# Experts' output products with the weights stationary, and gates spread over partitions through memory

## The reference, cut to what matters

```python
# layer 1: 8 experts, 64 -> 256 -> 64, each token goes to one expert, with a capacity
y = sum over e of gate1[t, e] * (relu(x @ w1[e] + b1[e]) @ w2[e])  +  gate1[t] @ b2
# NaN and infinities of y are replaced, then x = layer_norm(x + y)
# a two-layer gated recurrence along the 64 tokens of a row, x = layer_norm(x + h)
# layer 2: 16 experts, 64 -> 128 -> 64, each token goes to its two best experts
y = sum over e of gate2[t, e] * (relu(x @ w1[e] + b1[e]) @ w2[e])  +  gate2[t] @ b2
# x = layer_norm(x + layer_norm(x + y) * gamma + beta)
```

## Time and profile before

| | |
|---|---|
| Time before, median of 3 runs | 3099.89 us (3096.33 to 3101.36) |
| The profiled execution | 3111.34 us, span 3109.5 us |
| PE busy | 2843.0 us (91%) |
| PE weight loads busy | 1838.0 us (59%) |
| DVE busy | 2121.2 us (68%) |
| ACT busy | 2004.1 us (64%) |
| POOL busy | 61.8 us (2%) |
| Granted TensorE clock, mean | 0.962 of full speed |

### The profile page before, as it was taken

How to read it: one execution, slowest core, us unless ns; L and a number is a source line. 1 busy time by engine, 2 the same in 40 slices (tenths; PEclk the granted TensorE clock), 3 DMA queues, 4 the chain that set the end, 5 groups by cost and what they waited for, 6 DMA issues and landing times.

```text
span 3109.5 us, 78718 instructions
## 1 busy us (share of the span) xinstructions
PE 2843.0 (91%) x30194; PEld 1838.0 (59%) x30194; DVE 2121.2 (68%) x4213; ACT 2004.1 (64%) x2417; POOL 61.8 (2%) x81
## 2 busy tenths in 40 slices
PE   5777789999889999889999779999999999999997
PEld 3444456666656666556666534444444437888886
DVE  6999668888658888668888534445445435757855
ACT  5888656777546777556777457777777774444531
POOL 0000000000000000000000020000000001000000
PEclk9999899999999999999999889999999999999965
DMA  3432347644436654546544424111111100000000
GB/s 100 123 116 94 115 146 227 212 174 173 154 129 222 205 182 177 161 151 220 200 175 180 140 63 96 58 48 48 58 48 48 58 0 1 1 1 4 1 4 7
DMA packets 110842, 335.82 MB, mean 108 GB/s; under 512 B 46774, under 2 KB 74710, under 8 KB 74838
## 3 DMA queue, kind: packets, MB, share of 16 engines
q1 hardware_dynamic: 88150, 161.45, 16.6%
q10 hardware_dynamic: 18432, 134.23, 10.6%
q0 software_dynamic: 4096, 37.75, 5.7%
HBM read 179.24 MB, written 154.14 MB: 107 GB/s over the span
## 4 chain that ended last, share of the span: by engine, by line
PE 79%; DVE 7%; issue 6%; ACT 5%; DMA 2%; ACTq 0%; SPq 0%; DVEq 0%
PE pA L1436 15%; PE pA L1444 8%; PE pT L1531 8%; PE pS L1473 7%; PE pD L1520 4%; PE pD L1487 4%; PE pD L588 4%; PE pT L1462 3%; PE pA L588 3%; PE pD L1407 3%; PE pD L1502 3%; PE pS L574 2%; PE pT L574 2%; DVE arena L1803 2%; PE pA L1462 2%
## 5 line engine op out<-in xcount | busy, mean ns | idle before, releaser
L1770 DVE TENSOR_REDUCE small<-arena 128x32 f32<-128x1056 f32 x320 | 396.5, 1241 | 322.1 <-ACT arena L1605 318.6
L1436 PEld LDWEIGHTS pA<-conv_bd,h_in 128*128 128x128 f32 x4096 | 481.6, 193 | 108.1 <-issue 108.1
L1436 PE MATMUL pA<-conv_bd,h_in 128*128 128x128 f32 x4096 | 520.2, 281 | 2.0 <-DVE arena L1763 1.7
L1595 ACT COPY w_sb<-pA 128x1024 f32<-128x1024 f32 x256 | 259.4, 1013 | 251.8 <-PE pA L1444 233.6
L1616 ACT ACTIVATE h_new<-pT,bet,gam 128x1024 f32<-128x1024 f32 x256 | 307.1, 1199 | 155.2 <-PE pT L1462 138.2
L1784 DVE SCALAR_TENSOR_TENSOR w_sb<-w_sb,small 128x1024 f32<-128x1024 f32 x320 | 385.5, 1209 | 2.1
L1605 ACT ACTIVATE arena<-w_sb 128x1024 f32<-128x1024 f32 x320 | 338.6, 1058 | 10.2
L1473 PEld LDWEIGHTS pS<-cst,h_new 128*128 128x128 f32 x2048 | 222.5, 142 | 205.4 <-issue 132.7
L1462 PE MATMUL pT<-cst,w_sb 128*128 128x128 f32 x2048 | 280.4, 282 | 38.1 <-DVE w_sb L1784 20.3
L1473 PE MATMUL pS<-cst,h_new 128*128 128x128 f32 x2048 | 282.9, 282 | 25.2 <-ACT h_new L1616 22.6
L1462 PEld LDWEIGHTS pT<-cst,w_sb 128*128 128x128 f32 x2048 | 234.9, 145 | 103.7 <-DVE w_sb L1784 49.2
(11 more groups left out here) (300 smaller groups left out, 3919.2 us busy)
## 6 DMA issues: line engine op xcount, KB each, us to landing
h_scratch<-h_new ACTq DMA_DIRECT2D x128, 1024.0 KB, 4.4
h_in<-h_scratch SPq DMA_DIRECT2D x128, 1024.0 KB, 5.0
y_scratch<-w_sb POOLq DMA_DIRECT2D x32, 576.0 KB, 8.5
y_in<-y_scratch SPq DMA_DIRECT2D x512, 36.0 KB
w_sb<-in_L_tok_w1r_dram POOLq DMA_DIRECT2D x8, 576.0 KB, 6.9
w_sb<-in_L_tok_w1i_dram POOLq DMA_DIRECT2D x8, 576.0 KB, 6.8
w_sb<-in_L_tok_w2r_dram POOLq DMA_DIRECT2D x8, 576.0 KB, 7.0
w_sb<-in_L_tok_w2i_dram POOLq DMA_DIRECT2D x8, 576.0 KB, 6.9
```

The source lines that it names most:

```text
L1436: pe.matmul(pA[:, c:c + 128], h_in[:, 1024 * n + c:1024 * n + c + 128], conv_bd[:], start=(j == 0), stop=False, skip_group_check=True)
L1595: act.copy(raw[n], pA[:]).then_inc(s["copied"], 1)
L1770: dve.reduce_sum(var[n], sq[n % 2], axis=AX).then_inc(s["summed"], 1)
```

## The change

- `output` swaps its operands: `w2` of one block (128 x 64) is stationary, and 512 tokens of `hid` stream. The two halves k of a chunk go to partitions 0 to 63 and 64 to 127 of one bank, so the result has features on partitions. A step now covers both halves of an expert: layer 1 has 4 such products where there were 16, layer 2 has 2 where there were 8. `hidden` makes both halves in one step too, and holds 4 (layer 1) or 2 (layer 2) of the 8 `hid` buffers for each expert.
- The gate of a token must now lie along the free dimension, the same on 64 partitions. After `gt`, POOL stores the turned gates of a chunk to memory (`g1_dram`, `g2_dram`) and waits until they are there; SP then loads, for each expert, two broadcasts of 64 partitions x 512 tokens (pieces of 512 bytes) into one of 8 buffers `GB`. DVE waits for the buffer and multiplies by it. SP also loads the gates of the chunk once in compact form (`GE`) for `eb`.
- `eb` becomes two products, `b2` stationary and `GE` streaming. A new step `yb` turns the sum back to token-major with 4 transposes on PE; `post1` and `post2` read its bank. The guard moves ahead of it, onto the turned sum.
- `gru` on DVE joins two instructions into one. The stores of the results move from SP to POOL. 8 parameter loads fewer are made. `TOKEN_ORDER` is written anew.

```diff
@@ TOKEN_ORDER (start of it) @@
-    xt1.0 xt1.3 qkv.0 xt1.1 sc.0 ex.0 qkv.1 pt.0 sc.1 xt1.2 pv.0 qkv.2 ex.1 pt.1 wg.0 xt2.0 sc.2 ex.2 gl1.0 gx1.0 pt.2 pv.1 cum.0
-    pv.2 e1.0 e1.0 e1.0 e1.0 e1.0 xt2.1 e1.0 gt1.0 gl1.1 gx1.1 xt2.2 cum.1 qkv.3 gt1.1 e1.0 sc.3 e1.0 eb1.0 post1.0 e1.1 ex.3
+    xt1.0 qkv.0 xt1.1 sc.0 ex.0 qkv.1 pt.0 xt1.2 pv.0 qkv.2 xt1.3 xt2.0 sc.1 ex.1 sc.2 ex.2 gl1.0 pt.1 gx1.0 pt.2 cum.0 pv.1 qkv.3
+    gt1.0 e1.0 pv.2 e1.0 e1.0 xt2.1 e1.0 xt2.2 e1.0 e1.0 sc.3 gl1.1 e1.0 ex.3 gx1.1 e1.0 eb1.0 pt.3 wg.0 cum.1 gl1.2 yb1.0 pv.3
+    gt1.1 e1.1 e1.1 xt3.0 e1.1 gx1.2 gru0.0 xt2.3 e1.1 gru1.0 e1.1 gback.0 cum.2 e1.1 e1.1 xt4.0 gl1.3 gl2.0 gx2.0 gm2.0 e1.1
+    eb1.1 gt2.0 e2.0 e2.0 e2.0 e2.0 e2.0 e2.0 e2.0 yb1.1 e2.0 e2.0 gx1.3 e2.0 e2.0 xt3.1 e2.0 gru0.1 e2.0 cum.3 gru1.1 gt1.2 e2.0
...
+    e2.2 gl2.3 e2.2 e2.2 e2.2 gx2.3 gm2.3 e2.2 e2.2 e2.2 e2.2 gt2.3 e2.2 e2.2 eb2.2 e2.3 yb2.1 e2.3 e2.3 e2.3 e2.3 e2.3 e2.3 yb2.2
+    e2.3 e2.3 e2.3 e2.3 e2.3 e2.3 e2.3 e2.3 e2.3 eb2.3 yb2.3
@@ output, on PE @@
-                step(c, e, k, slot):
-                    for i in range(4):
-                        for h in range(H):
-                            mm = pe.matmul(b[:, S * (4 * k + i):S * (4 * k + i) + S],
-                                           hid[(slot + h) % 8][:, 128 * i:128 * i + 128], w2[:, (e * H + h) * S:(e * H + h) * S + S],
-                                           start=(h == 0), stop=(h == H - 1))
+                step(c, e, slot):
+                    for h in range(H):
+                        for k in range(2):
+                            mm = pe.matmul(b[64 * k:64 * k + 64, :], w2[:, (e * H + h) * S:(e * H + h) * S + S],
+                                           hid[(slot + H * k + h) % 8], start=(h == 0), stop=(h == H - 1))
@@ output_bias (eb) and turn_back (yb), on PE @@
-                    sent("d", pe.matmul(b[:], GT[c % 2][0:8 * E, :], b2[0:8 * E, :], start=True, stop=True))
+                    pe.wait_ge(s[f"ge{layer}{c % 2}_loaded"], 32 * (c // 2 + 1))
+                    for k in range(2):
+                        q = 64 * (c % 2) + 32 * k
+                        mm = pe.matmul(b[64 * k:64 * k + 64, :], b2[q:q + E, :], GE[layer - 1][c % 2][k][0:E, :], start=True, stop=True)
...
+                    for i in range(4):
+                        mm = pe.transpose(b[:, 128 * i:128 * i + 128], chunk(Y, c)[:, 128 * i:128 * i + 128], ident)
@@ combine, on DVE @@
-                        dve.tensor_tensor(by_tile(Z3[e % 2]), by_tile(b[:]), gv, ALU.mult).then_inc(s["td_free"], 1)
+                    dve.wait_ge(s[f"g_loaded{i % NGB}"], 32 * (i // NGB + 1))
...
+                        dve.tensor_tensor(Z3[e % 2], b[:], GB[i % NGB], ALU.mult).then_inc(s["td_free"], 1)
                         dve.tensor_tensor(y, y, Z3[e % 2], ALU.add)
@@ token_pool, for gt and yb2 @@
+                    pool.wait_ge(s["ts_free"], n_s + 4)
+                    pool.dma_start(dram[c], GT[c % 2][0:8 * E, :]).then_inc(s["gates_stored"], 16)
+                    pool.wait_ge(s["gates_stored"], 16 * GT_PLACE[int(key[0][2]), c])
...
+                    pool.wait_ge(s["acc_done"], c + 1)
+                    pool.dma_start(dst, chunk(X, c).rearrange("p (t x) -> p t x", x=S)).then_inc(s["out_stored"], 16)
@@ token_sp, for each expert and chunk in order @@
+                if (layer, c) not in begun:
+                    sp.wait_ge(s["gates_stored"], 16 * GT_PLACE[layer, c])
+                    for k in range(2):
+                        sp.dma_start(GE[layer - 1][c % 2][k][0:E, :].rearrange("e (t p) -> e t p", t=4), rows[k]).then_inc(s[f"ge{layer}{c % 2}_loaded"], 16)
+                if i >= NGB:
+                    sp.wait_ge(s["td_free"], freed[i - NGB] + 4)
+                for k in range(2):
+                    sp.dma_start(GB[i % NGB][64 * k:64 * k + 64, :].rearrange("d (t p) -> d t p", t=4),
+                                 rows[k, e].partition_broadcast(64)).then_inc(s[f"g_loaded{i % NGB}"], 16)
@@ gru, on DVE @@
-                    link(dve.tensor_scalar(GV, b[:], gbias[:, 2 * layer + 1:2 * layer + 2], 0.5, ALU.add, ALU.add))
-                    link(dve.tensor_tensor(GV, GV, GS, ALU.max))
+                    link(dve.scalar_tensor_tensor(out=GV, in0=b[:], scalar=half_bias[:, layer:layer + 1], in1=GS, op0=ALU.add, op1=ALU.max))
```

More of the change, by code:

```diff
@@ L203, in token_steps @@
             seen[op, c] = e + 1
-            units += [(int(op[1]), c, e, k) for k in range(2)]
-    slots = lambda layer: 2 if layer == 1 else 1
+            units.append((int(op[1]), c, e))
+    slots = lambda unit: 4 if unit[0] == 1 else 2
     steps, split, held, issued, out, slot = [], set(), 0, 0, 0, 0
@@ L212, in token_steps @@
             continue
[L213 to L224, removed]
+        while issued < len(units) and units[issued][0:2] in split and held + slots(units[issued]) <= 8:
+            layer, u, e = units[issued]
+            units[issued] += (slot,)
+            steps.append((f"hid{layer}", u, e, slot))
+            held += slots(units[issued])
+            slot = (slot + slots(units[issued])) % 8
+            issued += 1
+        layer, u, e, at = units[out]
+        steps.append((f"out{layer}", u, e, at))
+        held -= slots(units[out])
+        out += 1
     return steps
@@ L415, in build @@
         pick1, pick2, diff2, exp2 = ([tiny(w) for _ in range(2)] for w in (E2 * CT, E2 * CT, CT, CT))
-        inverse = tiny(CT)
+        inverse, half_bias = tiny(CT), tiny(2)
+        NGB = 8
+        GB = [w_sb[:, 2048 + 512 * i:2560 + 512 * i] for i in range(4)] + [w_sb[:, 6656 + 512 * i:7168 + 512 * i] for i in range(3)] + [h_in[:, 3584:4096]]
+        GE = [[[t[64 * j + 32 * k:64 * j + 32 * k + 32, 0:512] for k in range(2)] for j in range(2)] for t in (y_in, ge2)]
+        assert tiny_at[0] <= 6656
+        g1_dram = nc.dram_tensor("gates1_scratch", [NCH, CT * E1, P], F32, kind="Internal").ap()
+        g2_dram = nc.dram_tensor("gates2_scratch", [NCH, CT * E2, P], F32, kind="Internal").ap()
+        GT_PLACE, EB_FREED, sends_d = {}, {}, 0
+        for key in token_steps():
+            sends_d += TOKEN_SENDS.get(key[0], (0, 0))[0]
+            if key[0] in ("gt1", "gt2"):
+                GT_PLACE[int(key[0][2]), key[1]] = len(GT_PLACE) + 1
+            if key[0] in ("eb1", "eb2"):
+                EB_FREED[int(key[0][2]), key[1]] = sends_d + 4
         pA, pT, pD, pS = pb("pA"), pb("pT"), pb("pD"), pb("pS")
@@ L692, in hidden, with step, turn_gates @@
             def hidden(H, b1, **_):
[L694 to L697, removed]
+                def step(c, e, slot):
+                    for i in range(2 * H):
+                        q = e * H + i % H
+                        act.activation(hid[(slot + i) % 8], take()[:], ACT.Relu, bias=b1[:, q:q + 1]).then_inc(s["ts_free"], 1)
                 return step
-            def turn_gates(E, GT):
+            def turn_gates(layer, E, GT):
                 def step(c):
+                    if c >= 2:
+                        act.wait_ge(s["gates_stored"], 16 * GT_PLACE[layer, c - 2])
                     act.copy(GT[c % 2][0:8 * E, :], take()[0:8 * E, 0:P]).then_inc(s["ts_free"], 1)
@@ L868, in add_bias, with bias2, guard @@
                 own_freed()
-            def post1(c):
-                x, y = chunk(X, c), chunk(Y, c)
+            def bias2(c):
+                add_bias(c)
+                dve.sem_inc(s["mixed2"], 1)
+            turned = lambda b: b[:].rearrange("p (t h x) -> p t h x", h=2, x=S)
+            def guard(c):
+                add_bias(c)
+                y = chunk(Y, c)
                 I32 = mybir.dt.int32
@@ L942, in post2 @@
                 dve.sem_inc(s["acc_done"], 1)
-            do = dict(qkv=qkv, sc=sc, pv=pv, xt2=lower, xt4=lower, gl1=gl1, cum=cum, out1=combine(E1, gates1), out2=combine(E2, gates2),
-                      eb1=add_bias, eb2=add_bias, post1=post1, gru0=gru(0), gru1=gru(1), gback=gback, gl2=gl2, gm2=gm2, post2=post2)
+            do = dict(qkv=qkv, sc=sc, pv=pv, xt2=lower, xt4=lower, gl1=gl1, cum=cum, out1=combine(E1), out2=combine(E2),
+                      eb1=guard, eb2=bias2, yb1=post1, gru0=gru(0), gru1=gru(1), gback=gback, gl2=gl2, gm2=gm2, yb2=post2)
             dve.wait_ge(s["par_loaded"], 16 * N_PARAMS)
```

129 lines of the change are left out of this document (78 added, 51 removed).

## The result

The kernel before took 3098.11 us (median of 4 runs, 3092.86 to 3101.36), the changed one 3006.34 (4 runs, 2999.78 to 3009.09): a ratio of 0.9702, with a 95% interval of 0.968 to 0.9724. The profiled execution took 3009.09 us, 2.75 above the median.

A forecast was written before the change was run, and what follows sets the result against it. TensorE bound the token stage; VectorE would after the change. Start 2605 + VectorE with waits 412 + gates 6 + last store 5 = 3028 us span; + 2 - 11 = 3019, taken as 3020, range 2966 to 3086.

The forecast's parts named there:

- the forecast's own case: Token stage: cheaper output products pass the bound from TensorE to VectorE; time 3020 us, chance 0.52.
- The output products: TensorE, token stage: 1.87 us per layer-1 expert where 3.46 stood, 1.01 per layer-2 expert where 1.73 stood.
- the halves don't run side by side: Rival, output products: a pair costs 2.1 us instead of 1.73, 47 us more TensorE, about 3150 us; chance 0.03.
- The rest of an expert: Hidden products on TensorE: 0.98 us for four, 1.90 for layer 1's eight; whole experts 3.77 and 1.99 us.
- VectorE's need: Token stage from 2605 us: 329 us busy, divided by 0.92 for issue, makes 357 us.
- the prediction's own needs, 422 and 357: Token stage: TensorE's need before the change, at full clock, 422 us; VectorE's need after it, 357 us.
- The waits: Between engines in the token stage: 15% over VectorE's need as before, 357 x 1.155 = 412 us.
- The gates: Broadcast loads: hidden mid-chunk; 2 us each at three chunk starts, 6 us together, between 0 and 25.
- The rival that wanted them late for every expert: Gate loads don't overlap: 5.2 us a unit, VectorE waits for all 96, time 3113 us; chance 0.11.
- The tail: End of the kernel: POOL's last store takes between 2.6 and 8.5 us, taken as 5.
- PE cold all through layer 2: Rival: TensorE, waiting more often, runs layer 2 at 1.2 GHz, adding 125 us; time about 3081 us, chance 0.20.
- The order: Head of the token stage: `cum.0` ahead of chunk 1's attention may save up to 5 us, left as margin.

The follow-up runs named there:

- one half: Changed kernel with both halves' output products written to the same 64 partitions, instructions unchanged in number and size; 3076.76 us, 0.9914 of the kernel before.
- no low part: Changed kernel without the second hidden product of each pair (low part of the hidden weights); 3000.13 us, 0.9664 of the kernel before.
- Before, no guard: Kernel before without the guard's six instructions per chunk, which replace non-finite and huge values; 3080.84 us, ratio 0.9945.
- the order alone: Kernel before with the changed kernel's TOKEN_ORDER and nothing else; 3100.95 us, ratio 0.9976.

## Why the prediction was right, and where it was off

The time came out at 3006 where 3020 was forecast, and the forecast's own case happened: the output products got cheap, TensorE ceased to bind alone, the long cold stretches went. Counted as here the forecast stage was 3028 - 2567.9 = 460 us; it took 449.7. That the sum came so near is in part luck, as the waits show. Step by step:

- *The output products*: 1.87 and 1.01 us, right to the hundredth. That the halves don't run side by side is refuted by the run "one half": in turn they make the stage 70 us longer. That rival was priced too high, though: two products for one half take 1.79 us (half of 3.58) and not 2.1, and the time stays at 0.9914 of the kernel before where the rival had it slower.
- *The rest of an expert* was mis-sized: the hidden products behind a half-width pair take 1.12 to 1.14 us for four instead of 0.98. An expert takes 3.94 and 2.13 us instead of 3.77 and 1.99; 32 x 1.48 + 64 x 0.58 = 84.5 us of PE were saved at full clock, not 99. It did little harm, since 46 us of PE's time are worth only about 12.5 of the stage ("no low part").
- *VectorE's need*: 346.3 us of busy time in the stage, where 354.5 - 5.5 = 349.0 was foreseen (the 7 and the 2.8 of the sum only move work across the 2605 us at which it begins). The mixing product on dense gates takes 686 to 689 ns, as taken. That VectorE binds is not shown: taking 15 us of its work away changed no time that can be told from none. By the prediction's own needs, 422 and 357, the bound would have changed hands after 65 us of PE's 99, not 70.
- *The waits*: VectorE's idle time in the stage is 449.7 - 346.3 = 103.4 us, of which 32.0 are for gates, 10.2 the tail and 61 all else; the forecast had 460.1 - 349.0 = 111.1, of which 6 for gates, 5 for the tail and 100 for all else. So the waits between engines were taken 39 us too high, the gates and the tail 31 us too low. That these two errors nearly cancelled is luck.
- *The gates*, "in the middle of a chunk at nothing", was the step that failed in kind: it took issue (0.33 us) and landing (2.6) from loads and stores of other shapes. These loads take 0.62 and 6.9, and VectorE waited for them at six of the eight chunk starts and in six later experts. Their price is about 22 us of the stage. The rival that wanted them late for every expert didn't come: 12 waits for 96 experts.
- *The tail*: the store by POOL puts the end 10.2 us behind VectorE instead of 3.0. "Taken as 5" was too little, and 10.2 lies outside the 2.6 to 8.5 given for it.
- *The clock*: PE cold all through layer 2 didn't happen. From 2700 to 2900 the clock is 0.97, as in the kernel before; the difference lies behind, where that kernel stood at 0.57 from 2972 to 3092 and the changed one at 0.87 from 2900 to the end of its products at 2978. It dips to 0.50 for up to 14 us at a time, not only where PE had run out of work: from 2696 to 2702 PE is busy throughout. The prediction saw the clock come back when 512-column products took over the earlier trace rows. "Before, no guard" doesn't bear that out: there it came back at 3030 in the middle of the pattern of output products and weight loads in which the kernel before stayed at 0.50 from 3040 to 3092. What brings it back stays open.
- *The order* was priced at up to 5 us at the head. The head saved nothing: VectorE's first mixing product starts 52 us into the stage before, with the order alone and in the changed kernel. But with the new products the order is a condition of the gain: in the old order the same edits are worth 1.1%, not 3.0. The prediction had no term for that.

## What to carry to other kernels

When an edit cuts the work of the engine that binds, look for the gain in three more places before trusting the sum: the order written for the old balance, the transfers the edit adds (priced by a row of the same shape, pieces included), and the last store. A price read from the same form elsewhere in the same kernel (L1531 here) was right to the hundredth; a price taken from a transfer of another shape was off by more than a factor of two (2.6 and 6.9 us). And taking work from an engine that doesn't bind can still pay through TensorE's clock, as the guard's removal did in the kernel before (0.55% of the time).

## What the runs showed of the hardware

- Half-width products queue by half: four products issued half after half take the same 1.87 us as in turn, while four products for one half take 3.58.
- Loads that spread one row over 64 partitions land in 6.9 us in pieces of 512 bytes and in 3.2 us in pieces of 2 KB, with equal bytes and nearly equal issue time (0.62 and 0.60 us).
- An output store of 256 KB issued by POOL ended the program 10.2 us behind VectorE's last instruction, the same store issued by SP 3.05 us.
